# A Mamba and mixture-of-experts block: the helper work of the scan stage laid out anew over the items

## What is computed

```python
x = jnp.einsum('bld,ed->bel', hidden_states, in_proj_w)
xc = conv(x, conv_w)                      # 4 taps, per channel
x = silu(xc + conv_b[None, :, None])
x_dbl = jnp.einsum('bdl,ed->bel', x, x_proj_w)
dt_low, Bm, Cm = jnp.split(x_dbl, [dt_rank, dt_rank + d_state], axis=1)
dt = softplus(jnp.einsum('brl,dr->bdl', dt_low, dt_proj_w) + dt_proj_b[None, :, None])
A = -jnp.exp(A_log)
def step(state, inp):                     # over the 512 tokens
    d, b, c, u = inp
    state = state * jnp.exp(d[..., None] * A) + (d * u)[..., None] * b[:, None, :]
    return (state, jnp.einsum('bdn,bn->bd', state, c))
y = (ys + D[None, :, None] * x) * silu(z)
```

## Time and profile before

| what | value |
|---|---|
| median of 3 runs | 1153.71 us (1151.44 to 1154.50) |
| profiled execution, its own time | 1151.87 us |
| its span | 1150.2 us |
| busy shares | PE 81%, PEld 68%, DVE 64%, ACT 53%, POOL 52% |
| granted PE clock, mean | 0.916 |

### The profile page before, as it was taken

One profiled execution on the slowest core, in us unless ns is written; L12 is line 12 of the kernel. 1 busy time (PEld: TensorE's weight loads), 2 busy tenths in 40 slices (PEclk: granted clock), 3 DMA queues, 4 the chain that ended last, 5 costly groups with the idle time before them and its releaser, 6 DMA issues.

```text
span 1150.2 us, 22744 instructions
## 1 busy us (share of the span) xinstructions
PE 926.7 (81%) x5388; PEld 777.4 (68%) x5389; DVE 734.1 (64%) x1031; ACT 607.8 (53%) x1026; POOL 592.4 (52%) x521
## 2 busy tenths in 40 slices
PE   4439887789679877687499998979999999983787
PEld 2126656566567656575389997869888888872676
DVE  3737779877897779879854447634444455444457
ACT  1358797779976897879131122333434444432211
POOL 4137679666977689778500103722334444341164
PEclk9759998999989999889799999989999999996689
DMA  6201411151013301211120013756466646653377
GB/s 203 79 0 33 179 57 33 33 183 56 27 37 135 102 29 58 91 38 47 34 97 36 36 56 110 286 183 200 149 223 218 222 158 224 220 206 121 106 215 245
DMA packets 67432, 137.08 MB, mean 119 GB/s; under 512 B 9392, under 2 KB 15024, under 8 KB 67248
## 3 DMA queue, kind: packets, MB, share of 16 engines
q1 hardware_dynamic: 57696, 105.74, 28.0%
q0 software_dynamic: 8960, 29.37, 7.1%
q10 hardware_dynamic: 720, 1.31, 0.5%
HBM read 163.53 MB, written 42.07 MB: 179 GB/s over the span
## 4 chain that ended last, share of the span: by engine, by line
PE 38%; issue 4%; DVE 4%; POOL 3%; DMA 1%; ACT 1%; ACTq 0%; DVEq 0%; SPq 0%; POOLq 0%
PE psY L917 11%; PE psG L881 11%; PE psU L881 10%; PE psT L874 3%; POOL slot_in L609 3%; PE psHT L895 2%; ACT xh L1205 1%; DVE x_tok L1755 0%; DMA gbuf<-slot_out,posi 0%; PE dbu_ps L756 0%; DVE hl L1567 0%; PE y_ps L774 0%; DVE xl L1573 0%; DVEq L1732 0%; POOL gbuf L656 0%
## 5 line engine op out<-in xcount | busy, mean ns | idle before, releaser
L564 POOL TENSOR_TENSOR prod<-hst,cbc 128x512 f32<-128x512 f32 x256 | 327.7, 1305 | 104.1 <-PE y_ps L774 92.9
L1393 DVE TENSOR_TENSOR_SCAN hst<-dA,dbu_ps 128x512 f32<-128x512 f32 x256 | 302.1, 1206 | 75.3 <-PE dbu_ps L756 57.0
L756 PE MATMUL dbu_ps<-ident,dbuT 128*128 128x128 f32 x1024 | 171.2, 293 | 63.3 <-DVE hst L1393 44.9
L756 PEld LDWEIGHTS dbu_ps<-ident,dbuT 128*128 128x128 f32 x1024 | 124.7, 149 | 130.3 <-DVE hst L1393 84.8
L1103 ACT ACTIVATE dA<-dts,Aneg 128x512 f32 (+1 forms) x256 | 172.3, 712 | 59.8 <-DVE hst L1393 59.5
L1211 ACT CAST hh<-psHT 128x384 fp32r<-128x384 f32 x79 | 37.8, 478 | 290.0 <-PE psHT L895 290.0
L1114 ACT ACTIVATE dbuT<-duT,BT 128x512 f32 (+1 forms) x256 | 163.0, 708 | 1.9 <-PE dbu_ps L756 1.9
L774 PE MATMUL y_ps<-ident,prod 128*128 128x128 f32 x1024 | 159.9, 282 | 1.3 <-POOL prod L564 1.3
L881 PE MATMUL psG<-weights,xh 128*128 (+1 forms) x560 | 142.1, 337 | 14.9 <-issue 8.7
L917 PE MATMUL psY<-weights,hh 128*128 (+3 forms) x420 | 136.7, 407 | 16.4 <-DVE hl L1567 14.6
L881 PE MATMUL psU<-weights,xh 128*128 (+2 forms) x560 | 142.7, 337 | 0.0
(11 more groups left out here) (175 smaller groups left out, 1396.3 us busy)
## 6 DMA issues: line engine op xcount, KB each, us to landing
raw_gu<-in_L_ffn_w_gate_up_dram SPq DMA_DIRECT2D x100, 704.0 KB
raw_d<-in_L_ffn_w_down_dram SPq DMA_DIRECT2D x50, 512.0 KB
cbc<-c_rows SPq DMA_DIRECT2D x64, 256.0 KB, 3.1
slot_in<-ztile SPq DMA_DIRECT2D x3, 4096.0 KB, 13.6
gbuf<-slot_in SPq DMA_DIRECT2D x48, 256.0 KB, 3.2
slot_out<-yout POOLq DMA_DIRECT2D x48, 256.0 KB, 3.3
raw_d<-in_L_ffn_w_down_dram SPq DMA_DIRECT2D x50, 192.0 KB
xn_rows<-xin SPq DMA_DIRECT2D x16, 256.0 KB, 2.0
```

The lines of the kernel that those rows point to most:

```text
L564: pool.tensor_tensor(prod[:, prod_slot(n, j), :], hst[:, slot_of(n, j), :], cbc[:, n % 2, :], ALU.mult).then_inc(prod_ready, 1)
L756: last = tr(dbu_ps[j % 2][:, t * P:(t + 1) * P], dbuT[:, n % 2, t, j * P:(j + 1) * P], ident[:])
L1393: V.tensor_tensor_scan(hst[:, slot_of(n, j), :], dA[:, slot_of(n, j), :], dbu_ps[j % 2][:], 0.0, ALU.mult, ALU.add).then_inc(scanned, 1)
```

## The change

The same operations with the same operands are issued at other items. PE: `in_proj` of group 3 goes from item 9 to item 8; the eight conv_proj matmuls of group 0 from items 8 to 15 to items 9 to 16, and those of group 2 from 24 to 31 to 23 to 30; the four z blocks from items 17, 19, 21 and 23 to 19, 20, 21 and 22; `in_proj` of group 1 from item 18 to one matmul each at 20 and 22; the two context blocks from 32 and 34 to 31 and 33; `x_proj` from two matmuls each at 37 and 38 to one each at 35 to 38. DVE: the taps go from items 11 to 14 and 20 to 23 to every second item from 10 and from 24, `conv_to_sbuf` of group 0 from 16 to 18, `round_part` from j = 2 to j = 3. POOL's `log_part` follows it. ACT: `z_to_time` from items 24, 26, 28 and 30 to 27 to 30, in the last batch item from behind n = 6 and n = 7 to the same items; `silus` from item 39 to 38, and in it silu of z ahead of the wait for the convolution; `softplus_parts` from j = 0 of n = 12 to 15 to j = 2 of n = 11 to 14.

```diff
@@ -563,7 +563,7 @@
                     pool.wait_ge(prod_used, i + 1)
                     pool.tensor_tensor(prod[:, prod_slot(n, j), :], hst[:, slot_of(n, j), :], cbc[:, n % 2, :],
                                        ALU.mult).then_inc(prod_ready, 1)
-                    if bp is not None and 10 <= n < 14 and j == 2:
+                    if bp is not None and 10 <= n < 14 and j == 3:
                         log_part(bp, n - 10)
 
             for j in range(ND):
@@ -691,12 +691,14 @@
                     last = tr(dst[:, t * P:(t + 1) * P], ctx_cur[:, t, k * P:(k + 1) * P], ident[:])
                 last.then_inc(full, 1)
 
-            def in_proj(k, use, j):
-                bank_free(k, use)
-                for c in range(NK):
+            def in_proj(k, use, j, c0=0, c1=NK):
+                if c0 == 0:
+                    bank_free(k, use)
+                for c in range(c0, c1):
                     last = mm(mp[k][:], winT[:, c, j * P:(j + 1) * P], ctxT[:, c, PADC:PADC + L],
                               start=c == 0, stop=c == NK - 1)
-                last.then_inc(misc_full[k], 1)
+                if c1 == NK:
+                    last.then_inc(misc_full[k], 1)
 
             def conv_proj(k, use, j, m):
 
@@ -778,28 +780,26 @@
             def pieces(b, n, j):
 
                 bp = b + 1
-                m = n % 2 * ND + j
-                if 2 <= n < 4:
-                    conv_proj(0, base0(b), 0, m)
-                elif 6 <= n < 8:
-                    conv_proj(0, base0(b) + 5, 2, m)
-                if 4 <= n < 6 and j % 2 == 1:
-                    t = n % 2 * 2 + j // 2
-                    z_transposes(base0(b) + 1 + t, b, t)
-                if (n, j) == (2, 1):
+                i = n * ND + j
+                if i == 8:
                     in_proj(1, base1(b), 3)
-                if (n, j) == (4, 2):
-                    in_proj(1, base1(b) + 1, 1)
-                if n == 8 and j % 2 == 0:
-                    bank_free(1, base1(b) + 2 + j // 2)
-                    ctx_transposes(b + 2, j // 2, mp[1], misc_full[1])
-                if (n, j) == (9, 1):
-                    x_proj(xp_use(bp), bp, 0, 2)
-                if (n, j) == (9, 2):
-                    x_proj(xp_use(bp), bp, 2, ND)
+                if 9 <= i < 17:
+                    conv_proj(0, base0(b), 0, i - 9)
+                if 19 <= i < 23:
+                    z_transposes(base0(b) + 1 + i - 19, b, i - 19)
+                if i in (20, 22):
+                    in_proj(1, base1(b) + 1, 1, i // 2 - 10, i // 2 - 9)
+                if 23 <= i < 31:
+                    conv_proj(0, base0(b) + 5, 2, i - 23)
+                if i in (31, 33):
+                    k = (i - 31) // 2
+                    bank_free(1, base1(b) + 2 + k)
+                    ctx_transposes(b + 2, k, mp[1], misc_full[1])
+                if 35 <= i < 39:
+                    x_proj(xp_use(bp), bp, i - 35, i - 34)
                 if 10 <= n < 14 and j == 0:
                     dt_proj(dt_use(bp) + n - 10, n - 10)
-                if (n, j) == (10, 0):
+                if i == 40:
                     b_transposes(bt_use(bp), bp)
                 if 12 <= n < 16 and j == 1:
                     du_transposes(dut_use(bp) + n - 12, bp, n - 12)
@@ -842,8 +842,8 @@
                 for j in range(ND):
                     step(NB - 1, n, j)
                     add_y(NB - 1, n * ND + j - LAG)
-                    if 4 <= n < 6 and j % 2 == 1:
-                        t = n % 2 * 2 + j // 2
+                    if 19 <= n * ND + j < 23:
+                        t = n * ND + j - 19
                         z_transposes(base0(NB - 1) + t, NB - 1, t)
             for m in range(ITEMS - LAG, ITEMS):
                 add_y(NB - 1, m)
@@ -1054,15 +1054,25 @@
 
             def silus(bp, conv_done):
 
-                act.wait_ge(*conv_done)
-                nc.scalar.activation(xs[:].rearrange("p j l -> p (j l)"), xs[:].rearrange("p j l -> p (j l)"),
-                                     ACT.Silu).then_inc(silu_done, 1)
-                act.wait_ge(ln1_dve, 4 if isinstance(bp, int) else 8)
-                for j in range(ND):
-                    tile = bass.ds(bp * NL + j, 1)
-                    last = nc.scalar.activation(zs[:, j, :], x_tok[:, tile, :].rearrange("p a c -> p (a c)"),
-                                                ACT.Silu, bias=rs1[:, 4, tile], scale=rs1[:, 3, tile])
-                last.then_inc(silu_z, 1)
+                def silu_x():
+                    act.wait_ge(*conv_done)
+                    nc.scalar.activation(xs[:].rearrange("p j l -> p (j l)"), xs[:].rearrange("p j l -> p (j l)"),
+                                         ACT.Silu).then_inc(silu_done, 1)
+
+                def silu_of_z():
+                    act.wait_ge(ln1_dve, 4 if isinstance(bp, int) else 8)
+                    for j in range(ND):
+                        tile = bass.ds(bp * NL + j, 1)
+                        last = nc.scalar.activation(zs[:, j, :], x_tok[:, tile, :].rearrange("p a c -> p (a c)"),
+                                                    ACT.Silu, bias=rs1[:, 4, tile], scale=rs1[:, 3, tile])
+                    last.then_inc(silu_z, 1)
+
+                if isinstance(bp, int):
+                    silu_x()
+                    silu_of_z()
+                else:
+                    silu_of_z()
+                    silu_x()
                 nc.scalar.preload_act_table_set("natural_log_exp_and_others")
 
             def softplus_parts(bp, j):
@@ -1115,24 +1125,27 @@
                                                 scale=par(BT, b)[:, t, RK + n:RK + n + 1])
                 last.then_inc(dbut_ready, 1)
 
-            def step(b, n, bp=None):
+            def step(b, n, bp=None, z_use=None):
                 for j in range(ND):
                     decay(b, n, j)
                     if j == 2:
                         input_terms(b, n)
                     if bp is not None:
                         pieces(bp, n, j)
+                    t = n * ND + j - 27
+                    if z_use is not None and 0 <= t < NL:
+                        z_to_time(b, t, z_use + t)
 
             def pieces(bp, n, j):
                 b = bp - 1
-                if 6 <= n < 8 and j % 2 == 0:
-                    t = n % 2 * 2 + j // 2
-                    z_to_time(b, t, base0(b) + 1 + t)
-                if (n, j) == (9, 3):
+                i = n * ND + j
+                if 27 <= i < 31:
+                    z_to_time(b, i - 27, base0(b) + 1 + i - 27)
+                if i == 38:
                     silus(bp, (misc_read[0], base0(b) + 7))
-                if 12 <= n < 16 and j == 0:
-                    softplus_parts(bp, n - 12)
-                if 14 <= n < 16 and j == 2:
+                if 11 <= n < 15 and j == 2:
+                    softplus_parts(bp, n - 11)
+                if 14 <= n < 16 and j == 1:
                     du_to_time(bp, n - 14)
                 if n == 0 and j < 2:
                     du_to_time(bp, j + 2)
@@ -1179,10 +1192,7 @@
                 return lambda w: w[:, buf]
 
             for n in range(2, NS):
-                step(NB - 1, n)
-                if 6 <= n < 8:
-                    for t in range(n % 2 * 2, n % 2 * 2 + 2):
-                        z_to_time(NB - 1, t, base0(NB - 1) + t)
+                step(NB - 1, n, z_use=base0(NB - 1))
 
                 if n == 8:
                     act.wait_ge(skip_added, NB)
@@ -1411,28 +1421,26 @@
 
             def pieces(b, n, j):
                 bp = b + 1
-                if (n, j) == (2, 3):
+                i = n * ND + j
+                if i == 10:
                     dve.wait_ge(skip_added, bp)
                     dve.sem_inc(wait_carrier, 1)
-                    conv(1, base1(b), 3, 0, 2 * b + ND)
-                if n == 3 and j < 3:
-                    conv(1, base1(b), 3, j + 1, 2 * b + ND)
-                if (n, j) == (4, 0):
+                if i in (10, 12, 14, 16):
+                    conv(1, base1(b), 3, (i - 10) // 2, 2 * b + ND)
+                if i == 18:
                     conv_to_sbuf(0, base0(b), 0)
-                if (n, j) == (5, 0):
-                    conv(1, base1(b) + 1, 1, 0, 2 * b + ND + 1)
-                if n == 5 and j > 0:
-                    conv(1, base1(b) + 1, 1, j, 2 * b + ND + 1)
-                if (n, j) == (8, 0):
+                if i in (24, 26, 28, 30):
+                    conv(1, base1(b) + 1, 1, (i - 24) // 2, 2 * b + ND + 1)
+                if i == 32:
                     conv_to_sbuf(0, base0(b) + 5, 2)
-                if n == 8 and j % 2 == 1:
-                    use = base1(b) + 2 + j // 2
-                    ctx_to_sbuf(j // 2, mp[1], (misc_full[1], use + 1), misc_read[1])
-                if (n, j) == (9, 3):
+                if i in (33, 35):
+                    k = (i - 33) // 2
+                    ctx_to_sbuf(k, mp[1], (misc_full[1], base1(b) + 3 + k), misc_read[1])
```

(5 more changed lines are left out.)

## The result

The changed kernel takes 1163.84 us (median of 4 runs, 1162.43 to 1165.24) against 1152.96 us for the kernel before on the same chip: ratio 1.0094 with a 95% interval from 1.0075 to 1.0114. It is slower by 10.9 us, where 4.6 us were worked out and 1158 forecast. The profiled execution after is the slowest of its four (1165.24) and the one before lies under its median, so the two profiles differ by more, 13.4 us in span.

A forecast was written before the change was run, and what follows sets the result against it. Scans were taken as bound by a loop of hand-offs with no engine full. 3·(3.6 + 1.9 − 2.0) − 5.9 = +4.6 us on 1151.9 gave 1156.5, set to 1158 for the runs' median; own range 1151 to 1165, overall 1148 to 1167.

The forecast's parts named there:

- Items 8 to 31, +3.6: Scans 8 to 31 of each looped batch item: 41.6 us of work plus 8.0 of waits and clock, against 46.1.
- the clock term: Items 8 to 31: TensorE's lowered clock behind the first new gap only, 0.6 us per looped batch item.
- the 3.8 of item 23: Wait for the last zT copy before conv_proj: 3.1 us worked out, taken as 3.8 given the earlier slow conv pair.
- the taps' cover, 2.6: Taps of items 20 to 23 moved beside conv matmuls: 4·0.64 = 2.6 us saved per looped batch item.
- Items 32 to 39, +1.9: Context block waits at item 33, x_proj for silu of x: 16.2 us against 14.25 per looped batch item.
- three items at 1.74: Items 32 to 39: three scan items, TensorE-bound with one matmul each, priced at 1.74 us apiece.
- Items 40 to 63, −2.0: Softplus and rounding moved: first rounding's 1.97 us wait goes, GpSimd keeps 8.5 per n; −2.0 per looped batch item.
- The last batch item, −5.9: zT copies come singly, one stop of over 5 us instead of two; ScalarE carries the gain, −5.9 us.
- My second rival: TensorE runs at 1.2 GHz behind every new gap: +8.7 us more, 1167 us; chance 0.15.
- the first (no loop closes): z blocks and zT copies hold TensorE no longer than before: faster, 1141 us, or 1150 halfway; chance 0.22.
- The third (the tail gives nothing): Items 40 to 63 gain nothing because GpSimd had the pace all along: +6, 1164 us; chance 0.13.
- The fourth (no effect): Whole kernel: gains and losses cancel within 3.5 us, last batch item paying for the three: 1154 us; chance 0.15.

The follow-up runs named there:

- e6: Changed kernel with context blocks back at items 32 and 34 and silu of x ahead of silu of z: 1177.66 us, ratio 1.0006 to the kernel before.
- e4: Kernel before with only group 1's four taps moved to items 24, 26, 28 and 30, beside conv matmuls: 1151.25 us, ratio 0.9983.
- e10: Kernel before with early zT copies (looped batch items), changed last batch item, changed softplus and rounding, and group 1's taps beside conv matmuls: 1157.99 us, ratio 0.9845.
- e3: Changed kernel with silu of x put ahead of silu of z in the looped batch items: 1158.34 us, ratio 1.005 to the kernel before.
- e2: Kernel before with only the change's new places for softplus and the rounding: 1150.74 us, ratio 0.9988.
- e1: Kernel before with the new z block and zT copy places in the last batch item only: 1144.11 us, ratio 0.991.
- e7: Changed kernel with the looped batch items' zT copies ahead of the input terms, behind decays 25 (three) and 27: 1173.20 us, ratio 0.9964 to the kernel before.
- e8: Kernel before with the looped batch items' zT copies behind decays 24, 25, 27 and 29: 1169.37 us, ratio 0.9927.
- e11: As e10, but the last batch item's z blocks stay at items 17, 19, 21, 23, copies behind decays 24, 25, 27, 29: 1152.84 us, ratio 0.979.

## Why the prediction was wrong

The direction and the chain of causes were right, and the size was under half: 4.6 worked out, 10.9 measured. Step by step, by the sum 3·(3.6 + 1.9 − 2.0) − 5.9:

- *Items 8 to 31, +3.6.* Measured +4.7 (50.8 against 46.1). The first wait is 2.25 for 2.2, scans 8 to 18 are 17.64 against the 17.6 that the prices give, and scans 18 to 24 are 18.7 to 19.1. What failed is the clock term: "half a microsecond more (0.6) for the lowered clock behind the first gap", and the 0.7 that the 3.8 of item 23 has over the 3.1 of its wait, for a slow first conv pair. Without these 1.3 the prices sum to 48.4, and the same order at the full clock takes 48.3 (e6). So items and waits were right within 0.1, and the clock cost 2.5 us a batch item in the profile after, not 1.3: the rows show steps of 1.06 behind the second z block and behind the conv matmul in the same batch item, and the granted clock of the stretch at 0.93 to 0.97. The worth of the taps' cover, 2.6, was wrong too, though the sum didn't use it: alone it is 0.48 (e4) and beside the early copies 0 (e10).
- *Items 32 to 39, +1.9.* Measured +2.7. The wait of item 33 (2.9 for the item; 3.43, 3.85 and 2.98 from scan to scan) was seen, but "then x_proj and step 1.5" and "three items at 1.74" took x_proj at the price of another matmul: it is 2.01 an item, 0.8 for the three. That silu's order is 1.7 of the 1.9 holds only at the full clock (1.5, e3 against the changed kernel). The fall behind the context wait, 1.7 more in e3 (17.07 against 15.40), was not in the sum; it takes the place of the wait for silu and doesn't add to it.
- *Items 40 to 63, −2.0.* Measured −1.5 (−1.3 alone, e2). The lengths fit the mechanism that was told, GpSimd's pace, with 8.70 in place of 8.5 for an n; no run changed that pace.
- *The last batch item, −5.9.* Measured −7.2 in scans 18 to 28 and −8.5 us in time alone (e1). The stop at item 20 was taken over from before and is shorter, 4.95 from scan to scan in place of 7.00.
- *The sum.* Three errors of 1.1, 0.8 and 0.5, each tripled, are 7.2 us, less 1.3 for the last batch item: 5.9 against the 6.3 us missed. So close an agreement is in part luck: the stretches are from one profile of each kernel, and the profiles differ by 2.5 us more than the medians. The steps that failed are therefore two sizes in the stretches that recur: the clock term of items 8 to 31 (1.3 taken, 2.5 measured) and the price of x_proj (1.74 taken, 2.01 measured, three times). My second rival had the clock at +2.9 a batch item and was nearer in its total (1167, measured 1164) than the forecast, but not in its places: the falls came behind the second z block, the conv matmul and the context block, and none behind block 3 or x_proj.

Of the rivals, the first (no loop closes) fell with the first wait; e7 shows what it would have taken. The third (the tail gives nothing) fell by e2's window; that its total, 1164, is what was measured is luck. The fourth (no effect) falls by the interval of the ratio, 1.0075 to 1.0114. The rule of the Trainium skill on the idle array (TensorE: Matmul & The Clock Gate, What's actually happening) agrees with the windows after in part: I had kept it to the longest gap, and of the gaps of 2.25, 2.35 and 2.89 us one, two and three of three had a fall beside them. The page lets the level hang on how busy the array was of late and not on each gap, so "by the rule all three waits would be followed by half speed" said more than it does, and e6, with the same waits of 2.25 and 2.89 in three batch items, shows no fall there. The rule on the shared port (SBUF — State Buffer, Who interferes with whom) agrees with du at 1.76 right behind the rounding and with GpSimd's products at 6.09 for 5.18; that is argued from the durations, and no run took the port away.

## What to carry to other kernels

A helper that releases a single bank should stand ahead of long work on the engine that has a lead, and let that engine wait: the same four copies, moved ahead of the input terms, are worth 9 us in the kernel before and 15 to 18 in the changed one. When a loop body is priced, give every new gap on TensorE like those of 2.25 to 2.9 us seen here its clock as well as its length, as a range from nothing to the 1.4 to 1.7 us that a fall cost here, and multiply by the trip count before calling a term small. Before a part is priced from two profiles, compare stretches at the same granted clock. Two waits that lie side by side must be undone together, and a run that undoes one of them says nothing of its price.

## What the runs showed that I had not expected

The same gap on TensorE, to 0.01 us, is followed by the slow clock in one batch item and not in the next: behind the 2.35 us ahead of the context block the transposes took 1.11 us in the second batch item and 0.66 in the third of one execution. By the granted clock in the traces, the gap of 2.25 us had a fall beside it in 3 of 15 batch items (the five kernels with that order), the one of 2.89 in 8 of the same 15, and the one of 2.35 in 9 of 12. What decides is not shown: no run changed it alone. So windows of one kernel come in steps: scans 24 to 32 of the kernel before are 15.35, 16.73 or 17.03, and 12.95 in all three batch items once the gap is gone (e8). In e8 to e11, without gaps of over 1.2 us there, the clock stays at 1.00 from scan 8 to 40 in all twelve batch items.

The stretch with no edit, scans 0 to 8, varied by 3.9 us in sum between the fourteen profiles, and the last batch item's scans 28 to 60 from 43.2 to 47.5, so differences of some 4 us between two single profiles prove nothing on this kernel unless they are located in the edited stretch.
